# Macaron block on one core: the first feed-forward's down projection as three products of high and low halves

## The reference

```python
def fp4_linear(x, w):
    xq = fp4_quant_dequant(x)
    wq = fp4_quant_dequant(w)
    return jnp.einsum('bsk,nk->bsn', xq, wq)
gate = fp4_linear(x, w_gate)          # 256 -> 704
y = fp4_linear(x, w_up)               # 256 -> 704
h = jax.nn.silu(gate) * y
return fp4_linear(h, w_down)          # 704 -> 256
...
x = x + 0.5 * _L0_ffn_ref(_layernorm(x), ...)    # the kernel's stage S = 0
x = x + _L0_attn_ref(_layernorm(x), ...)         # stage 1
x = x + 0.5 * _L0_ffn_ref(_layernorm(x), ...)    # stage S = 2
x = x + 0.5 * _L1_ffn_ref(_layernorm(x), ...)    # stage 3
x = x + _L1_attn_ref(_layernorm(x), ...)         # stage 4
x = x + 0.5 * _L1_ffn_ref(_layernorm(x), ...)    # stage 5
```

## Time and profile before

| | us |
|---|---|
| median of the 3 runs | 2700.19 |
| lowest and highest | 2698.34, 2704.23 |
| the profiled execution: its own time | 2709.44 |
| its span, first to last instruction | 2707.5 |
| PE busy in the span | 2564.1 (95%) |
| DVE, ACT, POOL busy | 1842.8 (68%), 1338.6 (49%), 1042.5 (39%) |

### The profile page before, as it was taken

The page is one execution under the profiler, slowest core; times in us unless marked ns, Lnnn a source line. Parts: engine busy times, 40 slices in busy tenths (PEclk is TensorE's granted clock), DMA queues, the critical chain, the costliest instruction groups (busy, mean ns, idle before and its releaser), DMA issues.

```text
span 2707.5 us, 75841 instructions
## 1 busy us (share of the span) xinstructions
PE 2564.1 (95%) x31464; PEld 2155.4 (80%) x31464; DVE 1842.8 (68%) x4318; ACT 1338.6 (49%) x2217; POOL 1042.5 (39%) x1254
## 2 busy tenths in 40 slices
PE   4999999999999989999999899989999999979999
PEld 3878788778888878877887788877888888858888
DVE  7888788656766778888786566645555666546664
ACT  4444444333343334434443688854444554418886
POOL 5555555412121135545554333212344444453221
PEclk9999999989999999999999999989999999979999
DMA  5000000001111110000000000000000000000001
GB/s 179 1 6 1 1 1 1 1 15 23 23 23 22 25 47 1 1 1 1 1 1 1 17 1 1 1 12 18 17 17 18 17 17 17 19 4 24 32 32 40
DMA packets 67557, 45.85 MB, mean 17 GB/s; under 512 B 13184, under 2 KB 66192, under 8 KB 67216
## 3 DMA queue, kind: packets, MB, share of 16 engines
q1 hardware_dynamic: 67216, 41.00, 5.6%
HBM read 15.78 MB, written 8.40 MB: 9 GB/s over the span
## 4 chain that ended last, share of the span: by engine, by line
PE 65%; issue 13%; POOL 10%; DVE 7%; ACT 4%; DMA 0%; POOLq 0%; DVEq 0%; ACTq 0%
PE ps L575 12%; PE ps L46 8%; PE ps L48 7%; PE ps L47 7%; PE ps L1381 4%; PE ps L1382 4%; PE ps L1396 3%; PE ps L1398 3%; PE ps L599 3%; PE ps L248 3%; PE ps L930 2%; PE ps L1018 2%; DVE XTL L258 2%; POOL a1pry L1950 2%; POOL a1pry L1952 2%
## 5 line engine op out<-in xcount | busy, mean ns | idle before, releaser
L575 PE MATMUL ps<-WDT,fHT 128*128 128x256 f32 (+1 forms) x1536 | 386.1, 394 | 8.7 <-ACT fHT L626 8.7
L575 PEld LDWEIGHTS ps<-WDT,fHT 128*128 128x128 f32 (+1 forms) x1536 | 283.4, 192 | 82.5 <-issue 42.9
L1448 DVE TENSOR_TENSOR gHl<-gHf,gHh 128x512 fp32r<-128x512 f32 x256 | 190.7, 745 | 209.9 <-ACT gHh L1425 209.5
L46 PE MATMUL ps<-WGH,XTH 128*128 128x512 f32 (+1 forms) x768 | 313.1, 408 | 4.1 <-ACT fSG L632 1.7
L708 POOL TENSOR_TENSOR fV<-fH,frc 128x704 f32<-128x704 f32 x128 | 178.2, 1392 | 343.0 <-DVE frc L697 343.0
L48 PE MATMUL ps<-WGL,XTH 128*128 128x512 f32 (+1 forms) x768 | 289.7, 377 | 0.0
L47 PE MATMUL ps<-WGH,XTL 128*128 128x512 f32 (+1 forms) x768 | 289.1, 376 | 0.0
L217 POOL TENSOR_SCALAR ve<-mv 128x4 f32<-128x4 f32 x96 | 23.0, 240 | 633.9 <-DVE mv L209 630.2
L1396 PE MATMUL ps<-W2T,gHh 128*128 128x256 f32 x1024 | 257.2, 284 | 0.0
L1398 PE MATMUL ps<-W2T,gHl 128*128 128x256 f32 x1024 | 254.4, 280 | 0.0
L685 DVE TENSOR_TENSOR fH<-ps,fSG 128x704 f32<-128x704 f32 x128 | 113.6, 887 | 168.2 <-ACT fSG L632 155.6
(11 more groups left out here) (230 smaller groups left out, 6315.0 us busy)
## 6 DMA issues: line engine op xcount, KB each, us to landing
X<-in_x SPq DMA_DIRECT2D x16, 512.0 KB, 8.9
a0vp<-a0vt SPq DMA_DIRECT2D x256, 32.0 KB, 2.3
a1vp<-a1vk SPq DMA_DIRECT2D x256, 32.0 KB, 2.2
out<-X SPq DMA_DIRECT2D x16, 512.0 KB, 2.9
tws<-in_w SPq DMA_DIRECT2D x2, 1024.0 KB, 7.6
WN<-in_wgu SPq DMA_DIRECT2D x3, 384.0 KB, 5.4
a0km<-in_wqkv SPq DMA_DIRECT2D x2, 384.0 KB, 3.3
a1pry<-in_aw SPq DMA_DIRECT2D x1, 768.0 KB, 4.6
```

What stands on the lines that cost most here:

```text
L46: e.matmul(o, hh, mh, start=first, stop=False)
L575: h = pe.matmul(down, HT[n % 2][0:m, c, :], WDT[0:m, c, :], start=(c == 0), stop=(c == 5))
L1448: dve.tensor_tensor(Hl[m % 8][:, :], Hf[m % 4][:, :], Hh[m % 8][:, :].bitcast(F32), ALU.subtract).then_inc(s_hl, 1)
```

## The change

1. **Down projection.** `WDT` and `HT` (f32) are replaced by `WDH`/`WDL` and `HTH`/`HTL`, and the six f32 products of a tile by six `mm3`, which are 18 fp32r products of 256 columns (`out(n)`).
2. **Making the halves of h.** ACT now makes two copies of `turned`: `HTH` (rounded to fp32r) and `HTF` (f32, a single buffer). A new instruction on POOL, the 128x768 subtraction `HTL` = `HTF` - `HTH`, runs in iteration n for tile n-3, behind `HX(n-2)` and ahead of `x_scaled`, `spread` and `x_value`.
3. **One tile later.** PE runs `out(n-5)` in iteration n instead of the product for tile n-4, and DVE adds it for tile n-5. `out` waits for the low half, for the copies of the tile after it (`s_he`), and for the addition before it. After the last tile PE alternates the last five `out` with the last three transposes.
4. **Weights.** `start_*` no longer makes the down weights. PE runs the 12 transposes in tiles 1 (eight) and 2 (four) of stage 0 (`down_pe`), ACT copies them to `WDH` (four and two instructions, `down_act`), DVE subtracts `WDL` (`down_dve`) and sets the PSUM zeros (memset, L709 of after) in tile 2. The first `up` waits for its own part of `WGL` only. `x_mag` of chunk 1 moves behind the first silu.
5. **Memory.** SBUF tiles are laid out anew. No wait belongs to that.

The core of the diff:

```diff
@@ ffn0_pe
-                if 4 <= n < NT + 4:
-                    q = t - 4
-                    pe.wait_ge(s_he, q + 1)
-                    for c in range(6):
-                        m = 128 if c < 5 else 64
-                        h = pe.matmul(down, HT[n % 2][0:m, c, :], WDT[0:m, c, :], start=(c == 0), stop=(c == 5))
-                    h.then_inc(s_dn, 1)
+            def out(n):
+                pe.wait_ge(s_hlo, tb + n + 1)
+                pe.wait_ge(s_he, tb + min(n + 2, NT))
+                if n:
+                    pe.wait_ge(s_xd, 64 * S + n)
+                for c in range(6):
+                    m = 128 if c < 5 else 64
+                    h = mm3(pe, down, HTH[n % 2][0:m, c, :], HTL[n % 2][0:m, c, :], WDH[0:m, c, :], WDL[0:m, c, :],
+                            c == 0, c == 5)
+                h.then_inc(s_dn, 1)
...
+                if n >= 5:
+                    out(n - 5)
+                if n in (1, 2) and S == 0:
+                    for g in ((0, 1), (2,))[n - 1]:
+                        down_pe(pe, g)
...
+            for n in range(NT - 5, NT):
+                out(n)
+                if n + 2 < NT and n + 2 >= NT - 3:
+                    turn(n + 2)
@@ ffn0_act
                 if 3 <= n < NT + 3:
                     q = t - 3
                     act.wait_ge(s_ht, q + 1)
                     if n > 4:
                         act.wait_ge(s_dn, q - 1)
-                    act.activation(HT[(n - 3) % 2][:, :, :].rearrange("p c t -> p (c t)"), turned,
-                                   ACT.Copy).then_inc(s_he, 1)
+                    act.activation(HTH[(n - 3) % 2][:, :, :].rearrange("p c t -> p (c t)"), turned, ACT.Copy)
+                    if n > 3:
+                        act.wait_ge(s_hlo, q)
+                    act.activation(HTF[:, :, :].rearrange("p c t -> p (c t)"), turned, ACT.Copy).then_inc(s_he, 1)
@@ ffn0_dve
-                if 4 <= n < NT + 4:
-                    dve.wait_ge(s_dn, t - 3)
+                if n >= 5:
+                    dve.wait_ge(s_dn, t - 4)
...
+                if n in (1, 2) and S == 0:
+                    for g in ((0, 1), (2,))[n - 1]:
+                        down_dve(dve, g)
+                    if n == 2:
+                        dve.wait_ge(s_wl, 9)
+                        dve.memset(PSA[64:128, 3712:3840], 0.0).then_inc(s_hz, 1)
@@ ffn0_pool
+                if 3 <= n < NT + 3:
+                    pool.wait_ge(s_he, t - 2)
+                    if n > 4:
+                        pool.wait_ge(s_dn, t - 4)
+                    pool.tensor_tensor(HTL[(n - 3) % 2][:, :, :], HTF[:, :, :], HTH[(n - 3) % 2][:, :, :].bitcast(F32),
+                                       ALU.subtract).then_inc(s_hlo, 1)
```

More of the change, by code:

```diff
@@ L110, in macaron @@
[L110 to L122, removed]
@@ new lines, in macaron @@
+        rc = [sb(f0, f"frc{i}", [P, 44]) for i in range(2)]
+        turned_sb = f0.enter_context(ExitStack())
+        HTH = [sb(turned_sb, f"fHTH{i}", [P, 6, P], R32) for i in range(2)]
+        HTL = [sb(turned_sb, f"fHTL{i}", [P, 6, P], R32) for i in range(2)]
+        HTF = sb(turned_sb, "fHTF", [P, 6, P])
+        turned_sb.close()
+        WN = sb(f0, "WN", [P, 11, D])
+        WDN = sb(f0, "WDN", [P, 2, NF])
+        f0.close()
+        a0A = [sb(lay0, f"a0A{i}", [P, 1024]) for i in range(2)]
@@ new lines, in macaron @@
+        Vt = [sb(lay0, f"a0vt{i}", [P, D]) for i in range(3)]
+        a0KP = [sb(lay0, f"a0kp{i}", [P, D]) for i in range(2)]
+        a0YT = [sb(lay0, f"a0YT{i}", [P, D]) for i in range(2)]
+        sb(lay0, "gap1", [P, 288])
+        KM = [sb(lay0, "a0km0", [P, 2, 1024]), KMb]
+        QP = [sb(lay0, "a0qp0", [P, 2, 512]), QPb]
+        a0WH = sb(lay0, "a0wh", [P, 2, 768], R32)
+        a0WL = sb(lay0, "a0wl", [P, 2, 768], R32)
+        a0WO = sb(lay0, "a0wo", [P, 2, D])
+        bq = sb(lay0, "a0bq", [P, 4])
@@ new lines, in macaron @@
+        bm = sb(lay0, "a0bm", [P, 4])
+        bvt = sb(lay0, "a0bv", [P, D])
+        bot = sb(lay0, "a0bo", [P, D])
+        pw = sb(lay0, "a0pw", [16, 256])
+        rev = sb(lay0, "a0rev", [P, P])
+        g1 = sb(lay0, "a0g1", [16, 4])
+        DT = sb(lay0, "a0DT", [P, 2, 4, 64])
+        KD = sb(lay0, "a0KD", [P, 16])
+        GQ = sb(lay0, "a0GQ", [P, 2, 64])
+        bdp = sb(lay0, "a0bdp", [P, 32])
+        par25 = sb(lay0, "a0par", [P, 2])
+        VP = [sb(lay0, f"a0vp{i}", [P, 2, D]) for i in range(2)]
@@ L148, in macaron @@
         sx = [sb(a1, f"a1sx{i}", [P, 16]) for i in range(3)]
+        S0 = sb(a1, "a1s0", [P, 2, 64])
+        a1S = [sb(a1, f"a1S{i}", [P, 2, 64]) for i in range(4)]
+        PRY = sb(a1, "a1pry", [P, 1536])
+        RC = sb(a1, "a1rc", [P, 10, 80])
+        a1WO = sb(a1, "a1wo", [P, 2, D])
+        MBC = sb(a1, "a1mb", [P, 2, 128])
+        TR = sb(a1, "a1tr", [P, 64])
+        ON = sb(a1, "a1on", [P, 2, 32])
         a1.close()
         lay1 = top.enter_context(ExitStack())
-        sb(lay1, "over", [P, 15960])
+        sb(lay1, "over", [P, 19744])
         W1T = sb(lay1, "W1T", [P, 2, FF], R32)
@@ L380, in macaron @@
         wcol = [(k, c0, min(4, 11 - c0)) for c0 in range(0, 11, 4) for k in range(2)]
-        wbank = [PS[(0, 1, 2, 6, 7)[s % 5]] for s in range(12)]
+        wbank = [PS[n] for n in (0, 1, 2, 6, 7, 6)]
         def start_dve(dve):
@@ L561, in up @@
                     pe.wait_ge(s_hm, t)
+                if n == 0 and S == 0:
+                    pe.wait_ge(s_wl, 2 * c + 2)
                 for k in range(2):
@@ L585, in ffn0_pe @@
                     ffn1_set_pe(pe)
-                if n < NT and j in (2, 3):
+                if j in (2, 3):
                     x_turn_pe(pe, S, i + 1, j - 2)
[L588 to L604, removed]
+                if j == 0:
+                    pe.wait_ge(s_xl, 2 * (16 * S + i) + 2)
+                up(n, 0)
+                if n >= 3:
+                    turn(n - 3)
+                up(n, 1)
+                up(n, 2)
+            for n in range(NT - 5, NT):
+                out(n)
+                if n + 2 < NT and n + 2 >= NT - 3:
+                    turn(n + 2)
         def ffn0_act(act, S):
@@ L700, in ffn0_pool @@
             tb = 32 * S
-            for n in range(NT + 2):
+            for n in range(NT + 3):
                 t = tb + n
```

104 lines of the change are left out of this document (51 added, 53 removed).

## The result

The changed kernel takes 2732.81 us (median of 4 runs, 2731.94 to 2734.11), the kernel before, timed beside it, 2699.86 (4 runs, 2698.34 to 2704.23). The ratio is 1.012, 95% interval 1.0102 to 1.0137: slower by 1.2%, 33 us (28 to 37). I had forecast 2724, 24 us more: the result lies within my range of 2700 to 2750 and just above the 2715 to 2732 to which I gave the most. The profiled execution of after is 2731.94 us long (span 2730.0), at its own median; that of before stood 9.6 above its own.

What follows compares the result with a forecast made beforehand. PE bound the kernel before (95% busy); the ring and POOL's subtraction would hold the tiles after. Steady groups 17.8, last groups -3, tails 6.2, start 3: +24 us, median 2700.2 to 2724, range 2700 to 2750.

Steps and rivals of the forecast that it cites:

- The ring: Chain from one H to the next through DVE, ACT's mag, copies and silu: 6.66 us, 7.35 with the second copy.
- The subtraction and its queue: POOL's new 128x768 subtraction takes 1.83 us (bounds 1.46 to 1.93) and delays x_scaled, so x transposes start 3.19 behind H.
- r = 2 and r = 3: The two tiles with x transposes in each steady group of four: 8.44 and 8.30 us instead of 7.87.
- PE's gain: Down projection: 18 fp32r products take 2.1 us against 2.88 for twelve f32 instructions, saving about 0.8 us a tile.
- the last case of the third rival: PE stays the bound in every tile: -95 us, 2605 us; chance 10% together with every tile at 7.35.
- Start: First tiles of the program: delays up to H of tile 3 and the next group, +3 us, bounds -4 and +5.
- 17.8 - 3: Steady tiles of both stages: 24 groups at 0.74 us more, +17.8; the last two groups of each stage, -3.
- Tail of S = 0: Each stage's end, where PE alternates products and transposes: +3.1 us a stage, +6.2 together; bounds +2 and +5 a stage.
- the clock: Rival: PE's wait of some 1.6 us at r = 2 drops it to half clock; +14 to +29 more, 2738 to 2753; 20%.
- No change: Rival: the subtraction is at its lower bound or below and the start gains 4 us: 2699 us; 12%.
- faster: Rival: x work fits beside POOL's subtraction, 2675 us, or PE stays the bound, 2605 us; together 10%.
- the first case of the third rival: POOL's subtraction doesn't hold up x_scaled and spread, every tile takes 7.35: -31 us, 2675 us; 10% with the 2605 case.

Runs made afterwards that it cites:

- second profile of before: The kernel before the change, profiled once more with no edit; measured 2704.56 us, profiled span 2702.2 us instead of 2707.5.

## Why the prediction was right, and where it was off

- **The ring.** 6.66 + 0.69 = 7.35 at r = 0 and 1: measured 7.29 and 7.36. It holds with the x work moved too (7.35 to 7.39 in all four), and without the second copy r = 0 and 1 fall to 7.07. Shown.
- **The subtraction and its queue.** 1.83 forecast, 1.84 measured; x transposes 3.19 against 3.20 behind H. Moving it took 47 us away; doubling it cost 204, part of it by the clock. Shown.
- **r = 2 and r = 3.** 8.44 and 8.30 forecast, 8.44 and 8.38 measured. At r = 3 norm starts 2.99 behind H (385.23 - 382.24) and not 2.81.
- **PE's gain.** 18 products at 0.118 were to take 2.1 us; they take 2.42 (381.98 to the x transposes at 384.40). The row from which I took 0.118 has 128-row weights; at the 64-row weights of the last block the starts lie 0.21, 0.22, 0.13 and, up to the x transposes, 0.20 apart:

```profile
383.64 0.28 PE L48 MATMUL ps<-WDL,fHTH 128*128 128x256 f32 x1
383.85 0.39 PE L46 MATMUL ps<-WDH,fHTH 64*128 64x256 f32 x1
384.07 0.28 PE L47 MATMUL ps<-WDH,fHTL 64*128 64x256 f32 x1
384.20 0.27 PE L48 MATMUL ps<-WDL,fHTH 64*128 64x256 f32 x1
384.40 0.66 PE L258 MATMUL ps<-ident,fXV 128*128 128x128 f32 x4
```

  0.46 a tile is saved and not 0.8. It did no harm, since PE had ceased to be the bound, but the last case of the third rival (PE stays the bound, 2605 us) was priced too low: 128 x 0.46 is 59 us and not 100.
- **The sum by place,** from the profiles of before (first) and after. Start: +1.3 at H of tile 3 (forecast +3). S = 0 from there to H of tile 63: +11.9. S = 2 from H of tile 0 to H of tile 63: +6.1; together 18.0 where my terms were 17.8 - 3. Tail of S = 0: +1.7, of S = 2: **+8.6**, forecast 3.1 each. With 0.3 less in the attention this is the 29.3 us at the end of S = 2, where I had 24.
- **One tile of S = 0 fell to half clock.** Tile 38, where PE also prepares the attention, took 10.75 us for 8.57 before: 0.57 of it is that of every r = 2, 1.6 is the clock. First the changed kernel, then the kernel with PE kept at work in the tails, which does the same here, has the same waits and takes 9.14:

```profile
343.92 0.66 PE L258 MATMUL ps<-ident,fXV 128*128 128x128 f32 x4 [0.27 <-ACT a0KD L870]
344.33 0.64 PE L46 MATMUL ps<-WGH,XTH 128*128 128x512 f32 x1
344.77 0.63 PE L47 MATMUL ps<-WGH,XTL 128*128 128x512 f32 x1
```

```profile
343.00 0.66 PE L258 MATMUL ps<-ident,fXV 128*128 128x128 f32 x4 [0.27 <-ACT a0KD L879]
343.42 0.47 PE L46 MATMUL ps<-WGH,XTH 128*128 128x512 f32 x1
343.73 0.39 PE L47 MATMUL ps<-WGH,XTL 128*128 128x512 f32 x1
```

  A wait of 1.21 us (1.20 in the second kernel) for x_scaled stands before it in both. In the first profile of before, tile 22 of S = 2 lost the same 1.6, so the two cancel in the sum.
- **The mis-sized term is the tail of S = 2.** I had priced blocks at half clock there as a bound of +5 a stage and took full clock. In each of three steps the block waits 1.65 to 2.23 us for the second copy, the transposes wait 0.56 to 1.60 for the addition, and all four blocks ran at half clock in part or whole. The kernel before ran this tail at 0.93; its tail of S = 0 was at 0.72 and 27.0 us long (window 530 to 560), so there the loss stood already. Against the forecast the tail of S = 2 is 5.5 us over and the steady tiles 3.2; the start (1.7) and the tail of S = 0 (1.4) are under. So errors of both signs cancel in part, and that the total came within 9 us is in part luck. The 3.6 us between the 29.3 of the traces and the 32.9 of the medians no stretch explains.
- **The offset of the profile.** At the end of S = 2 the two profiles differ by 29.3 us (30.6 against the second profile of before), at the end of the program by 22.5. I took the 9.2 us between profile and median as the same for both kernels. It is not: after's profile stands 0.9 below its median, and the untouched last stages varied by 7 us. 5 of these lie in the second attention, and they go with the clock: PE is busy 616.9 us there in the first profile of before, at a granted clock of 0.96, and 611.0 and 612.0 us in the other two, at 0.97. What makes the clock differ from one execution to the next is open.

The rivals: the clock did not fall in the steady r = 2 tiles, where I had put it at 20%, but in tile 38 of S = 0 and in the tails. One of the rows on which I rested that rival, 0.99 us behind a gap of 1.57, did not come again in the second profile of before, with the same gap. No change and faster did not happen; the first case of the third rival (every tile at 7.35) came true once the order in POOL's queue was changed, at 2685.8 us where it had 2675.

## What to carry to other kernels

When work is moved off the bound engine, the engine that gets the new instruction is to be checked for what stands behind it in its queue, not for its busy share: at 47% busy, 1.84 us in the wrong place cost more than the whole gain, and behind the x work it held up no tile. If the bound has moved, the cheaper instruction is worth nothing until the new bound is mended; replacing it by the dear one, as in the run with six f32 products, tells this at once. In the tails here, where PE alternates with other engines, the waits cost twice, once as time and once as clock.

## What the runs showed of the hardware

- The granted clock behind waits of PE: one of 1.20 us in each steady group left it at full (x transposes 0.66); one of 3.1 us brought it to 1.2 GHz in 20 of 24 groups (up to 1.12 for the same transposes) and left it at full in four.
- The same wait can go either way from one execution to the next: 1.57 us in tile 22 of S = 2 of the kernel before (0.99 and 0.66 for the transposes), 1.2 and 0.27 us in tile 38 of S = 0 of two kernels that differ in the tails alone (10.75 and 9.14 for the tile).
- In the tails, waits of 0.56 to 2.23 us between blocks came with a granted clock of 0.72 and 0.76; unit transposes put into them held it at 1.00 and made the two tails 11.3 us shorter.
- fp32r products of 256 columns start 0.118 us apart with 128-row weights, but 0.21, 0.22 and 0.13 at the change to 64-row weights and behind it, and 0.20 back to the next 128-row ones.
- A subtraction of 128x768 takes 1.84 us on POOL from SBUF and 0.94 on DVE from PSUM.
